# Loading only q, k and v ahead of the list of units, and the other weights piece by piece in its first three slots

## What is computed

```python
q, k = relu(x @ Wq) + 1e-3, relu(x @ Wk) + 1e-3         # A: 16 heads of 64, causal linear attention
attn = (q . cumsum(k v^T)) / (q . cumsum(k));  x + attn @ Wo + bo
x + (int8(x) @ int8(rhs)) * row_scale * rhs_scale       # F0: quantised product, rhs is 512 x 512
# B: 16 heads of 32; q, k, v = x @ q_w.T ...; rotary turn; q and k to rank 16 for each head;
M = M * sigmoid(logits) + (sigmoid(x @ g_w.T + g_b) * k) v^T;  y = q M;  layernorm(x + y @ out_w.T + out_b)
x + (int8(x) @ int8(rhs)) * row_scale * rhs_scale       # F1
```

## Time and profile before

| | us |
|---|---|
| median of 3 runs | 3245.57 (3244.02 to 3248.70) |
| profiled execution, its own time | 3244.64 |
| its span, first to last instruction | 3242.9 |
| first matmul of the list | at 119.06 |
| chunk 0's wo1 ends, in slot 2 | at 157.4 |
| chunk 1's wo1 ends, in slot 3 | at 186.8 |

### The profile page before, as it was taken

How to read it: one execution, slowest core, us unless ns; L and a number is a source line. 1 busy time by engine, 2 the same in 40 slices (tenths; PEclk the granted TensorE clock), 3 DMA queues, 4 the chain that set the end, 5 groups by cost and what they waited for, 6 DMA issues and landing times.

```text
span 3242.9 us, 104237 instructions
## 1 busy us (share of the span) xinstructions
PE 3108.5 (96%) x44242; PEld 2368.6 (73%) x44242; DVE 2179.4 (67%) x4675; ACT 564.6 (17%) x1048; POOL 1016.1 (31%) x1371
## 2 busy tenths in 40 slices
PE   1599999999999999999999999999999999999995
PEld 1577777777777777777777777777777777777774
DVE  7566766666766666666676676676676666666664
ACT  2111111111111111111111111111111111111111
POOL 0023333333333333333333333333333333333333
PEclk8799999999999999999999999999999999999998
DMA  4122222222222222222222222222222222222221
GB/s 164 50 43 46 40 47 44 40 47 44 40 47 44 47 42 46 46 43 46 46 40 46 46 40 47 44 40 47 44 40 47 44 45 44 44 46 44 46 39 26
DMA packets 383786, 151.88 MB, mean 47 GB/s; under 512 B 353312, under 2 KB 361632, under 8 KB 383392
## 3 DMA queue, kind: packets, MB, share of 16 engines
q1 hardware_dynamic: 383392, 145.56, 24.3%
HBM read 44.83 MB, written 16.78 MB: 19 GB/s over the span
## 4 chain that ended last, share of the span: by engine, by line
PE 95%; DVE 3%; DMA 1%; issue 1%; ACT 0%; POOL 0%; POOLq 0%; SPq 0%; DVEq 0%; ACTq 0%
PE bank L598 20%; PE bank L600 20%; PE bank L599 20%; PE bank L835 7%; PE bank L659 4%; PE bank L685 4%; PE bank L725 3%; PE bank L565 2%; PE bank L789 2%; PE bank L672 2%; PE bank L768 2%; PE bank L699 2%; PE bank L759 2%; PE bank L812 2%; PE bank L799 1%; DVE absmax L1016 1%
## 5 line engine op out<-in xcount | busy, mean ns | idle before, releaser
L598 PE MATMUL bank<-xaT,wq_hi 128*128 128x128 f16 x2048 | 358.6, 220 | 25.7 <-DMA xaT<-xa_split 25.7
L599 PE MATMUL bank<-xaT,wq_hi 128*128 128x128 f16 x2048 | 357.3, 219 | 0.0
L600 PE MATMUL bank<-xaT,wq_lo 128*128 128x128 f16 x2048 | 357.3, 219 | 0.0
L598 PE MATMUL bank<-xaT,wk_hi 128*128 128x128 f16 x2048 | 356.8, 219 | 0.0
L599 PE MATMUL bank<-xaT,wk_hi 128*128 128x128 f16 x2048 | 356.8, 219 | 0.0
L600 PE MATMUL bank<-xaT,wk_lo 128*128 128x128 f16 x2048 | 356.7, 219 | 0.0
L1105 DVE TENSOR_SCALAR work<-bank,eps_q 128x256 f32<-128x256 f32 x256 | 123.4, 482 | 330.4 <-PE bank L600 330.3
L553 POOL TENSOR_TENSOR xf<-xwb,xf 128x512 f32<-128x512 f32 x64 | 81.8, 1277 | 656.7 <-DVE xf L1185 656.7
L598 PEld LDWEIGHTS bank<-xaT,wq_hi 128*128 128x128 f16 x2048 | 200.6, 98 | 56.3 <-issue 48.6
L835 PE MATMUL bank<-wout,turn_q 128*128 128x512 f32 x512 | 233.8, 599 | 1.9 <-ACT turn_q L942 1.9
L530 POOL TENSOR_TENSOR turn_q<-turn_q,cross_q 128x512 f32<-128x512 f32 x64 | 104.5, 1632 | 334.5 <-DVE cross_q L1209 334.5
(11 more groups left out here) (203 smaller groups left out, 8220.6 us busy)
## 6 DMA issues: line engine op xcount, KB each, us to landing
xin<-in_L_attn_a_x SPq DMA_DIRECT2D x64, 256.0 KB, 2.6
out<-xf SPq DMA_DIRECT2D x64, 256.0 KB, 2.1
table<-in_tables SPq DMA_DIRECT2D x64, 192.5 KB, 2.9
work<-in_L_attn_a_Wq SPq DMA_DIRECT2D x1, 2048.0 KB, 7.8
work<-in_L_attn_a_Wk SPq DMA_DIRECT2D x1, 2048.0 KB, 14.0
work<-in_L_attn_a_Wv SPq DMA_DIRECT2D x1, 2048.0 KB, 7.5
work<-in_L_attn_a_Wo SPq DMA_DIRECT2D x1, 2048.0 KB, 8.4
work<-work SPq DMA_TRANSPOSE x128, 3.6
```

The lines of the kernel that those rows point to most:

```text
L598: nc.tensor.matmul(o, a[0], b[0], start=first, stop=False)
L599: nc.tensor.matmul(o, a[0], b[1], start=False, stop=False)
L600: return nc.tensor.matmul(o, a[1], b[0], start=False, stop=last)
```

## The change

Before the list only x of chunk 0, Wq, Wk and Wv are taken in, and chunk 0's norm, split and transpose (AHEAD) are put between them. v is loaded into what is later the tile of layer B's weights (wb_all). The other weights are cut into pieces (load, max, all, scale, hi, lo; for rhs max, all, round), and the table LATE says behind which unit of slots 0 to 2 each engine does its piece; "(1, qk1_e)" is slot 1, behind the place of qk1_e. A piece's load on SyncE waits until the weight whose room it takes is done (taken). TensorE waits for each weight at its first use (need). q_w, k_w, v_w, g_w, out_w and the rank weights come from the host transposed and laid out, so their 22 groups of transposes on TensorE, the evictions, and the spreading on VectorE go; out_w and the ranks are loaded straight to their place. The powers of the decay are made on GpSimd instead of VectorE. turn_q, turn_k, cross_q and cross_k become parts of "work", which grows from 8192 to 10240 elements. The counts of the bank waits have 1 setup unit in them instead of 23 (COUNTS, not shown).

```diff
-SETUP_UNITS = 23
+SETUP_UNITS = 1
...
+AHEAD = ("ld_x", "na_st", "na_rs", "na_ap", "xTa_h", "xTa_l", "xTa_t")
+
+LATE = {
+    (0, "qk0"): ("load o",),
+    (0, "qk2_e"): ("max o", "all o"),
+    (1, "qk3_e"): ("scale o", "hi o"),
+    (1, "s0_e"): ("lo o", "load rhs", "load bk"),
+    (1, "o0_e"): ("max rhs", "all rhs"),
+    (1, "o1_e"): ("max bk", "all bk"),
+    (1, "aT1_l"): ("scale bk", "hi bk", "round rhs", "load bq"),
+    (1, "qk1_e"): ("lo bk", "load g"),
+    (1, "qk2_e"): ("max bq", "all bq"),
+    (2, "wo_e"): ("scale bq", "hi bq", "max g", "all g"),
+    (2, "qk3_e"): ("lo bq", "load bv", "scale g", "hi g"),
+    (2, "s0_e"): ("lo g",),
+    (2, "s1_e"): ("max bv", "all bv"),
+    (2, "o0_e"): ("scale bv", "hi bv"),
+    (2, "o1_e"): ("lo bv",),
+}
+
+TAKEN = ("q", "k", "v", "o", "rhs", "bk", "bq", "g", "bv")
...
+        wb_all = sb("wb", [P, 6, KD * D], F16)
+        wb = {n: tuple(wb_all[:, 2 * i + half, :].rearrange("p (k n) -> p k n", k=KD) for half in range(2))
+              for i, n in enumerate("qkv")}
...
+        wide = {"q": work[:, 0:4096], "k": work[:, 4096:8192],
+                "v": wb_all[:, 0:4, :].rearrange("p h n -> p (h n)").bitcast(F32), "o": work[:, 6144:10240],
+                "rhs": work[:, 6144:8192], "bk": work[:, 8192:10240], "bq": work[:, 6144:8192],
+                "g": work[:, 8192:9216], "bv": work[:, 6144:8192], "out": work[:, 8192:10240]}
...
+                    j = slot.first - lag
+                    if name in steps and (slot.it is not None or (0 <= j < CHUNKS and (j > 0 or name not in AHEAD))):
                         steps[name](Chunk(slot, lag, full, empty, ps))
+                    if slot.it is None:
+                        for piece in LATE.get((slot.first, name), ()):
+                            if piece in late:
+                                late[piece]()
...
+            def load(n, src, free=None):
+                if free is not None:
+                    taken(sp, free)
+                sp.dma_start(in_rows(n, src), src.rearrange("(k p) n -> p k n", p=P)).then_inc(loaded[n], 16)
...
+            ld_x(first_chunk(sp, "ld_x"))
+            load("q", Wq)
+            with nc.allow_non_contiguous_dma(reason="1 KB of logits"):
+                sp.dma_start(logit[:, :], logits.rearrange("(j h) r -> (h r) j", j=2)).then_inc(s_logit, 16)
+            load("k", Wk)
+            load("v", Wv)
+            for row, src in ((bo_row, bo), (outb_row, out_b), (lng_row, ln_g), (lnb_row, ln_b), (gb_row, g_b)):
+                sp.dma_start(row[:, :], src.rearrange("(a n) -> a n", a=1).to_broadcast([P, src.shape[0]]))\
+                    .then_inc(s_row, 16)
+            xTa_t(first_chunk(sp, "xTa_t"))
+            for w, to in enumerate((rankq, rankk)):
+                sp.dma_start(to[:, :, :, :], ranks[w]).then_inc(s_rank, 16)
+            sp.dma_start(wout[:, :, :], out_w.rearrange("(k p) n -> p k n", p=P)).then_inc(s_wout, 16)
             run(sp, "SP", dict(ld_x=ld_x, ld_t=ld_t, st_o=st_o, xTa_t=xTa_t, aT0_t=aT_t(0), aT1_t=aT_t(1), xTb_t=xTb_t,
-                         qT0_t=qT_t(0), qT1_t=qT_t(1)))
+                         qT0_t=qT_t(0), qT1_t=qT_t(1)),
+                {"load o": lambda: load("o", Wo, "k"), "load rhs": lambda: load("rhs", rhs, "o"),
+                 "load bk": lambda: load("bk", k_w, "o"), "load bq": lambda: load("bq", q_w, "rhs"),
+                 "load g": lambda: load("g", g_w, "bk"), "load bv": lambda: load("bv", v_w, "bq")})
...
+            def powers_of(table, squares):
+                link(pool.memset(table[:, :, 0:1], 1.0))
+                for n in range(7):
+                    w = 1 << n
+                    link(pool.tensor_tensor(table[:, :, w:2 * w], table[:, :, 0:w],
+                                            squares[:, n, :, None].to_broadcast([P, 2, w]), ALU.mult))
+                    link(pool.tensor_tensor(squares[:, n + 1, :], squares[:, n, :], squares[:, n, :], ALU.mult))
+
+            def powers_of_decay():
+                pool.wait_ge(inverse_ready, 1)
+                powers_of(pow_i, squares_i)
+                powers_of(pow_d, squares_d)
+                pool.tensor_copy(decay128[:, :], squares_d[:, 7, :])
+                pool.tensor_tensor(q_decay[:, :, :], pow_d, squares_i[:, 6, :, None].to_broadcast([P, 2, P]), ALU.mult)
+                pool.tensor_tensor(k_decay_t, pow_i, squares_d[:, 6, :, None].to_broadcast([P, 2, P]), ALU.mult)\
+                    .then_inc(kdec_ready, 1)
...
+            all_of("q")()
+            inverse_std("a")(first_chunk(pool, "na_rs"))
+            all_of("k")()
+            powers_of_decay()
+            all_of("v")()
+            pool.wait_ge(s_row, 16 * 5)
...
+            def need(c, n):
+
+                if c.per == 0 and c.j == 0:
+                    taken(pe, n)
...
             def qk_(i):
+                    need(c, "k")
...
+            pe.wait_ge(s_pool, 9)
+            pe.wait_ge(kdec_ready, 1)
+            transposes(ps[0], lambda j: k_decay_t[:, j, :], 2, ident[:, :]).then_inc(full[0], 1)
...
+            def hi(n):
+                def piece():
+                    slot, src, (w_hi_, _) = WEIGHTS[n]
+                    act.wait_ge(wscale, slot + 1)
+                    nc.scalar.activation(w_hi_[:, :, :], in_rows(n, src), ACT.Copy, scale=scale[:, slot:slot + 1])\
+                        .then_inc(w_hi, 1)
+                return piece
...
+            hi("q")()
+            xTa_h(first_chunk(act, "xTa_h"))
+            hi("k")()
+            hi("v")()
...
+            def rest_of(n):
+                def piece():
+                    slot, src, (hi, lo) = WEIGHTS[n]
+                    dve.wait_ge(w_hi, slot + 1)
+                    dve.wait_ge(wscale, slot + 1)
+                    nc.vector.scalar_tensor_tensor(lo[:, :, :], in_rows(n, src), scale[:, slot:slot + 1], hi[:, :, :],
+                                                   ALU.mult, ALU.subtract).then_inc(s_read, 1)
+                return piece
...
+            def rest_of_bk():
+                link(nc.vector.tensor_scalar(k_decay[:, :], k_decay[:, :], unscale[:, SBK:SBK + 1], float(DB) ** -0.5,
+                                             ALU.mult, ALU.mult))
+                rest_of("bk")()
...
+            def round_rhs():
+                st = in_rows("rhs", rhs)
+                dve.wait_ge(rmax_all, 1)
+                link(nc.vector.tensor_scalar(rs_row[:, :], rhs_all, 1e-12, 1.0 / INT8_MAX, ALU.max, ALU.mult))
+                link(nc.vector.reciprocal(rhs_all, rs_row[:, :]))
+                link(nc.vector.tensor_tensor(st, st, rhs_all[:, None, :].to_broadcast([P, KD, D]), ALU.mult))
+                link(nc.vector.tensor_scalar(st, st, MAGIC, None, ALU.add))
+                nc.vector.tensor_scalar(rhs_q[:, :, :], st, -MAGIC, None, ALU.add).then_inc(s_read, 1)
...
+            head_masks()
+            max_of("q")()
+            inverse_of_decay()
+            na_st(first_chunk(dve, "na_st"))
+            scale_of("q")()
+            max_of("k")()
+            na_ap(first_chunk(dve, "na_ap"))
+            scale_of("k")()
+            rest_of("q")()
+            halve_x(first_chunk(dve, "xTa_l"))
+            max_of("v")()
+            rest_of("k")()
+            scale_of("v")()
+            scale_eps()
+            keep_decay()
+            rest_of("v")()
+            dve.wait_ge(s_row, 16 * 5)
...
+LAYOUT = {"L0_attn_b_q_w": by_head_pairs, "L0_attn_b_k_w": by_head_pairs, "L0_attn_b_v_w": transposed,
+          "L0_attn_b_g_w": transposed, "L0_attn_b_out_w": transposed}
```

More of the change, by code:

```diff
@@ L181, in read, with hybrid_kernel @@
         return self.ps[BANK[unit]], self.empty[BANK[unit]]
-def hybrid_kernel(nc, x, Wq, Wk, Wv, Wo, bo, q_w, k_w, v_w, Wqr, Wkr, g_w, g_b, logits, out_w, out_b, ln_g, ln_b,
-                  rhs, tables, keeps, out):
+def hybrid_kernel(nc, x, Wq, Wk, Wv, Wo, bo, q_w, k_w, v_w, g_w, g_b, logits, out_w, out_b, ln_g, ln_b,
+                  rhs, ranks, tables, keeps, out):
     ctx = ExitStack()
@@ L263, in hybrid_kernel @@
         recip_d = sb("recip_d", [P, 2, 2, 4])
-        work = sb("work", [P, 8192])
+        work = sb("work", [P, 10240])
         def part(at, *shape):
@@ L352, in hybrid_kernel, with first_chunk, run @@
         w_hi = sem("weights_hi")
-        kdec_used = sem("k_decay_used")
         rmax = sem("rhs_max")
         rmax_all = sem("rhs_max_all")
[L356 to L362, removed]
+        def first_chunk(eng, name):
+            return Chunk(Slot(eng, LAG[name]), LAG[name], full, empty, ps)
+        def run(eng, name_of, steps, late):
             def walk(slot):
                 for name, lag in ORDER:
-                    if name in steps and (slot.it is not None or 0 <= slot.first - lag < CHUNKS):
+                    j = slot.first - lag
+                    if name in steps and (slot.it is not None or (0 <= j < CHUNKS and (j > 0 or name not in AHEAD))):
                         steps[name](Chunk(slot, lag, full, empty, ps))
```

(46 more changed lines are left out.)

265 lines of the change are left out of this document (71 added, 194 removed), and 31 rows, old and new, of the table COUNTS.

## The result

| | before | after |
|---|---|---|
| median of 5 runs each | 3245.57 (3244.01 to 3248.70) | 3230.40 (3228.28 to 3232.19) |
| ratio, with its 95% interval | | 0.9953 (0.9938 to 0.9967) |
| span of the profiled execution | 3242.9 | 3226.0 |
| first matmul of the list | 119.06 | 53.2 |
| chunk 0's wo1 ends | 157.4 | 125.5 |

A forecast was written before the change was run, and what follows sets the result against it. TensorE's work was taken to bound the stream, with the 119.06 us before it paid in full. A gain of 50.4 us by chunk 0's wo1, less 7.2 in slot 2, left 43.2: 3245.6 - 43.2 = 3202.4, range 3192 to 3212.

The forecast's parts named there:

- What bounds the kernel, and the loop: Whole kernel: TensorE's work sets the stream of 64 chunks, the 119.06 us before it are paid in full; loop unchanged.
- rival D: Loop: buffers moved into work are slower there, each of 54 slots pays; 3256 at 1 us a slot; chance 0.03.
- Part 1: Before the stream: VectorE's order sets when q, k, v are ready; TensorE starts at 42.0, 77 us earlier; rest v ends 50.6.
- The port step: Powers on GpSimd: they and VectorE's rest q and rest k hold each other up at shared ports; 5.7 us.
- the long bound: Powers on GpSimd: each meeting waits for the other engine's whole instruction, k_decay ready at 41.4; short bound 5.7 us less.
- Part 2: Slots 0 and 1: 24.9 us of VectorE pieces plus waits; chunk 0's wo1 ends at 107.0, gain 50.4 us.
- Part 3: Slot 2: 11.4 us of pieces fit VectorE's time, only order costs; 7.2 us lost, gain 43.2.
- C: First slots: longer ramp, with rest k, the roundings and SyncE's loads each later; 3212 to 3235 us; chance 0.12.
- A: First slots, the forecast itself: early start, half eaten by the ramp; 3192 to 3212 us; chance 0.70.

The follow-up runs named there:

- the fourth run: Loads of bq, g and bv put behind the transposes and x load they had stood ahead of on SyncE, against the changed kernel; 3228.14 us, ratio 0.9946.

## Why the prediction was wrong, step by step

**What bounds the kernel, and the loop: right.** The gain is what the first slots leave of the earlier start, and nothing of rival D is seen: the turn and cross parts in "work" cost nothing (windows above).

**Part 1 failed, and it is the step that decides.** Its text has the all-reduce of k straight behind na_rs, the powers from 21.4 behind that, and v's all-reduce straight behind the powers: GpSimd's operations were summed by their own durations, with nothing between them. Four code changes lie there (8.47, 6.09, 7.38, 5.98). The first two put k's all-reduce at 30.81 where about 21.0 was forecast, 9.8 late (some of their 14.6 pass while VectorE still takes k's maximum); the third adds 7.4 and the fourth 6.0. The powers took 14.0 from start to end where 20.0 was forecast, and gave 6.0 back: 17.2 in all. VectorE's timeline after shows what they do:

```profile
24.82 0.55 DVE L1096 TENSOR_SCALAR xna<-xin,mean_var_a,rstd_a 128x512 f32<-128x512 f32 x1 [3.56 <-POOL rstd_a L559]
31.25 0.15 DVE L1016 TENSOR_SCALAR absall<-absall 128x1 f32<-128x1 f32 x1 [5.88 <-POOL absall L528]
...
41.21 4.47 DVE L1029 SCALAR_TENSOR_TENSOR wk_lo<-work,scale,wk_hi 128x4096 f16<-128x4096 f32 x1
59.03 0.15 DVE L1016 TENSOR_SCALAR absall<-absall 128x1 f32<-128x1 f32 x1 [13.35 <-POOL absall L528]
...
63.34 4.49 DVE L1029 SCALAR_TENSOR_TENSOR wv_lo<-wb,scale,wv_hi 128x4096 f16<-128x4096 f32 x1 [2.88 <-ACT wv_hi L905]
```

Scale k came at 31.25 (forecast 21.4), rest k ended at 45.7 (36.1), rest v at 67.8 (50.6): 17.2 late. The steps beside GpSimd were right: Wk (0.5 late) and Wv were there when VectorE wanted them, the powers' own work was 9.9 us (13.96 from 38.65 to 52.61, less the 4.1 for which one of them was held up) in place of 10.6, and VectorE's order cost what its rows said.

The port step was half right. The powers met k's rest, and one multiplication took 4.40 while that ran (41.44, issued 0.23 behind it): the long bound, a wait for the whole instruction, as the Trainium skill (SBUF — State Buffer, "Who interferes with whom") has it. The collision with q's rest, another 4.4 to 5, never came, because the code change held the powers back until 38.65. So one error hid part of another term.

**Part 2: right in its shape, and late by what part 1 was late.** Chunk 1's qk1_e ended at 112.9 in place of 95.4, that is 17.5 late, of which 17.2 were there at its start. The wait ahead of s1 came as forecast, 8.10 us for 7.5, and with it the lower clock. TensorE's timeline, and the windows of that stretch and of wo0:

```profile
86.76 1.65 PE L697 MATMUL bank<-work 64*128 64x128 f32 x12 [8.10 <-ACT work L933]
```

```profile
84.00:90.00 6.00, 3.24 (x60) 3.05 (x64) 2.44 (x5) 1.69 (x3) 0.69 (x2) 0.50 0.65 215
...
119.00:123.00 4.00, 4.00 (x11) 1.37 (x10) 0.33 (x1) 0.00 (x0) 0.35 (x1) 0.51 0.63 100
```

The granted clock was 0.50 and 0.51, the lower of the two levels, around the end of the first wait and behind the second (15.4 us). SyncE's queue held aT0 behind the load of bq, as written (and aT1 behind that of g, 116.06 behind 115.57):

```profile
111.35 0.38 SPq L421 DMA_DIRECT2D work<-in_L_attn_b_q_w  x1
111.85 1.24 SPq L448 DMA_TRANSPOSE work<-work  x1
```

wo1 ended at 125.5 in place of 107.0: 18.5 late, 1.3 of it new.

**Part 3 was too small: slot 2 loses 16.1 us (31.9 less 15.8), not 7.2.** TensorE waits twice there: 11.7 us ahead of s1, priced at 3.2, and 1.5 for u0_e, where 4.0 was priced. The rest is its clock, which part 3 left out of the sum (the range had "about 2" for it):

```profile
135.70:147.40 11.70, 0.04 (x2) 0.07 (x2) 5.32 (x13) 2.89 (x6) 1.49 (x4) 0.68 0.31 108
147.40:152.00 4.60, 4.60 (x92) 4.26 (x94) 3.97 (x8) 0.35 (x1) 0.00 (x0) 0.50 0.27 61
152.00:157.00 5.00, 5.00 (x121) 4.93 (x118) 2.26 (x9) 2.34 (x2) 0.41 (x1) 0.84 0.01 3
```

4.6 at half speed and 5.0 at 0.84 lose 2.3 and 0.8. 11.7, 1.5 and 3.1 make 16.3, against 16.1. The wait ahead of s1 is 8.5 longer than priced, and VectorE's timeline shows whence:

```profile
128.23 0.75 DVE L1164 SCALAR_TENSOR_TENSOR xwa<-bank,unscale_vo,xwa 128x512 f32<-128x512 f32 x1 [8.90 <-POOL xwa L565]
...
140.43 0.69 DVE L1088 BATCH_NORM_STATS2 stats_a<-xin 128x6 f32<-128x512 f32 x1 [4.36 <-DMA keep_a<-in_keeps]
...
145.48 0.55 DVE L1096 TENSOR_SCALAR xna<-xin,mean_var_a,rstd_a 128x512 f32<-128x512 f32 x1 [1.71 <-POOL rstd_a L559]
```

wo_e could have begun at 125.6, when wo1 ended, and begins 2.6 later, because GpSimd turns from all-reduces to bias only at 126.87. na_ap waits 1.71 for another turn, the 9.28 of which end at 143.72. Between them 4.36 pass in waiting for a queue that the text named for slot 1 and did not go through for slot 2: x of chunk 2 (ld_x) stands behind "load bv" on SyncE, which waits for bq's rest. 2.6, 4.4 and 1.7 make 8.7. But the 4.4 are not the queue's alone. With SyncE's order mended and nothing else (the fourth run), VectorE has x at once, and na_ap waits 5.46 for GpSimd's turn in place of 4.36 and 1.71:

```profile
144.04 0.55 DVE L1098 TENSOR_SCALAR xna<-xin,mean_var_a,rstd_a 128x512 f32<-128x512 f32 x1 [5.46 <-POOL rstd_a L561]
```

So it is the turn of GpSimd that holds this stretch, and the queue stands second behind it.

**The sum.** At the end of chunk 1's wo1 the forecast had 43.2 and the runs 15.8. Of the 27.4 us between them, part 1 is 17.2, part 2 another 1.3, and part 3 the last 8.9 (16.1 less 7.2).

**The rivals.** The time fell into C's range (3212 to 3235), which had 0.12, but not by C's mechanism: the roundings and k's rest took their time, and transposes landed as priced. Neither A nor any rival named GpSimd's own order. The earlier trace rows gave prices for operations of one kind only, and no row of before shows a change between kinds with nothing over it. The order in which the new GpSimd stream alternates stands in the diff; its price did not stand in any row.

## What to carry to other kernels

Where an edit mixes library operations of GpSimd (all-reduces) with ordinary ones, count the places at which the kind changes in program order, and price each at 6 to 10 us from the end of the operation before it, unless GpSimd waits longer there anyway. Group them, or give the few ordinary ones to another engine, even to one that is the busier: VectorE took the powers and the kernel gained 12.6 us. And when a load that waits is put into a queue, write down what is behind it in every slot, not only in the one that looks critical; a wait taken from TensorE there may only uncover the engine that was as late.

## What the runs showed of the hardware that was not expected

The price of a change depends on its direction and on what the DMA engines do. Windows over the gaps of the kernel after (the last two figures are the DMA share and GB/s), to ordinary, to library, to ordinary, then to ordinary in slot 2:

```profile
15.38:23.86 8.48, 0.00 (x0) 0.00 (x0) 5.30 (x8) 3.71 (x1) 0.01 (x1) 1.00 1.00 346
24.71:30.81 6.10, 0.00 (x0) 0.00 (x0) 0.55 (x1) 0.63 (x1) 0.01 (x2) 1.00 0.04 15
31.26:38.65 7.39, 0.00 (x0) 0.00 (x0) 7.29 (x7) 3.71 (x1) 0.01 (x2) 1.00 0.04 10
...
134.43:143.72 9.29, 1.25 (x6) 0.39 (x4) 4.71 (x13) 2.21 (x3) 0.01 (x2) 0.80 0.46 141
```

Over all gaps by "issue" of these kernels: with a DMA share up to 0.35 the way to an all-reduce took 5.7 to 6.6 and the way back to an ordinary operation 6.7 to 7.8 (once 8.6, at 0.34). With loads of 1 or 2 MB under way (share 0.38 and more) the first took 7.6 to 9.3 (and 10.5, share 0.79, ahead of the first all-reduce of the kernel with the eight additions) and the second 7.5 to 10.0, so the ranges of the first lie apart and those of the second touch. That loads and changes share a path is argued from this, not shown: no run changed the loads alone, and the page's DMA queues show no more bytes for the kernel with the eight additions than for the one before (145.56 and 6.19 MB on the two large ones in both).

An all-reduce of one column on GpSimd (0.41) took 4.52 beside a VectorE instruction with two SBUF inputs issued 0.18 ahead of it: the shared port holds up library operations too.
